# Quarter sums of the base weights made in the first phase and kept in DRAM; the second pair of token tiles takes seven products

## The chip, the cores and the metric

The kernel runs on one core of a Trainium2 chip, as one program. The metric is the device time in microseconds (us) of that core; lower is better. All data are fp32; matmul operands are split by hand into a high part (rounded to the type fp32r) and a low part (the rest), and a product is three fp32r matmuls: high by high, high by low, low by high.

## What is computed

A gated cross-attention block over `x` (4 batches of 512 tokens, width 1024), then a feed-forward part made of one base matrix and low-rank experts. The feed-forward part is what the change touches:

```python
x = x + tanh(g_xattn[0]) * xattn(layernorm(x), ctx, Wq, Wk, ...)      # first phase
x = x + tanh(g_ffn[0]) * ffn(layernorm(x), W_base, ...)               # last phase

def ffn(x, W_base, b_base, W_gate, W_thr, b_thr, A_w, B_w):
    base = einsum('bsd,od->bso', x, W_base) + b_base                  # 2048 x 1024 x 1024
    gate = softmax(xf @ W_gate.T)
    thr  = sigmoid(xf @ W_thr + b_thr[0]) * 0.125
    w    = relu(gate - thr), divided by its sum
    moe  = einsum('ner,ne,eor->no', xf @ A_w, w, B_w) * 2             # 8 experts, rank 16
    return base + moe
```

## The kernel before

**Stages.** One list of stages, `stages = first + last` (L334 to L440), is written out by hand. Every engine (TensorE, ScalarE, VectorE, GpSimd) and the DMA queue of SyncE walks the same list and does its own part of each stage, in that order; semaphores join them. So the place of a stage in the list fixes what is queued behind what on every engine.

**First phase (`first`).** In order: keys from the context (stages `k`, `k_out`, `k_low`, with the weights `wkf`, whose eight regions `r_wk` lie behind the context `ct`, L122); the products of the query weights with themselves (`g`, two sweeps of eight steps, brought out of PSUM by `g_out` into `gram`: ScalarE writes the high part, VectorE the low part); keys times query weights (`m`, eight rows, brought out by `m_out`); then for each of the four batches the row products `y` (eight per batch), scores, softmax and `attend`. Beside them run `x_stat` (statistics of the 16 token tiles of `x`, each loaded by SyncE two `x_stat` stages ahead, L788), and for batch `b` the chain `load_xt` (2 MB of transposed `x` in four quarters), `z` (VectorE scales a quarter, L1166), `zh` (ScalarE rounds it), `zl` (VectorE takes the rest, L1172). For batch 0 this chain stands inside the second `g` sweep; `load_xt` 0 waits until all key products are done (`p_k`, L797), because `x` transposed lies where `ct` and `wkf` lay. Row `m` r waits for `m_out` r-3 (L620), since three PSUM banks turn; `mr` 1, behind the first `y`, waits for the fourth `z` (L521).

**Last phase (`last`, L386 on).** The 2048 tokens are eight pairs of 128-token tiles. A pair p starts with `hd` (expert and gate logits, L701), takes its products with the base matrix, adds the expert part (`fin`), and is stored. The matrix is cut into quarters B11, B12, B21, B22 (1 MB each). A plain pair takes eight products (`PLAIN_PRODUCTS`), each of 12 matmuls of 128x512. Any other pair takes seven (`PRODUCTS`), with four sums of token quarters (s1 to s4) and four sums of weight quarters: T1 = B12 - B11, T2 = B22 - T1, T3 = B22 - B12, T4 = B21 - T2. `PLAIN = 2`: pairs 0 and 1 are plain, pairs 2 to 7 take seven. The token sums for the next pair are made by ScalarE and VectorE during the pair before (`zt`, `sum_high`, `sum_low`).

**Where the T's came from.** At the end of the first phase and in pairs 0 and 1 SyncE loads the raw quarters into the slots of the T's and a second copy beside them (`w_load`, L826). VectorE (T1, T2; L1326) and GpSimd (T4, T3; L1493) subtract half by half, ScalarE rounds the high half (`split`, L1053), VectorE takes the low (L1334). All this stands between the products of pairs 0, 1 and 2:

```python
PRODUCTS = [("P1", "a11", "B11", "A", True), ("P2", "a12", "B21", "B", True), ("P6", "s2", "T2", "A", False),
            ("P5", "s1", "T1", "C", True), ("P7", "s3", "T3", "A", False), ("P3", "s4", "B22", "C", False),
            ("P4", "a22", "T4", "D", True)]
```

Of the kernel before, what the change touches and what calls it, by code (L numbers as in the profile page):

```python
# [43 lines left out]
def build(nc, x, xt, ctx, ctxt, wq, wk, wb, hd, bt, vec, fn_w, b_base, scal, out):  # L44
# [9 lines left out]
    B = 4  # L54
# [10 lines left out]
    PLAIN = 2  # L65
# [3 lines left out]
    with ExitStack() as stack:  # L69
# [15 lines left out]
        def own(name, shape, dt=F32):  # L85
            n = WORD
            for s in shape[1:]:
# [33 lines left out]
                    for h, n in enumerate(("xth", "xtl")))  # L121
# [11 lines left out]
        EARLY, LATE = 2 * TPB, 3 * TPB  # L133
# [14 lines left out]
        xs = [at(f"xs{i}", [P, D], F32, o) for i, o in enumerate((r_kt + 2 * ROW, r_kt + 3 * ROW, r_xa, r_xa + ROW))]  # L148
# [7 lines left out]
        wh, wl, w_raw, w_tmp = ({op: at(f"{n}_{op}", [P, KH, HALF], dt, o + h * SLOT // 2) for op, o in w_at.items()}  # L156
                                for n, dt, h in (("wh", F32R, 0), ("wl", F32R, 1), ("wr", F32, 1), ("wx", F32, 0)))
# [162 lines left out]
        for p in range(NP):  # L320
# [8 lines left out]
            for i, (n, z, *_) in enumerate(products(p)):  # L329
                if all(z != z_ for _, z_, *_ in products(p)[i + 1:]):  # L330
# [14 lines left out]
        for r in range(KB):  # L345
            first += [("m", r), ("m_out", r)] + [("x_stat", EARLY + r - 2)] * (1 < r < 6)
        first += [("load_xt", 1), ("load_fn", 0), ("load_xa", 0), ("load_xa", 1), ("load_bb",)]
        for b in range(B):
            for j in range(FB):
# [10 lines left out]
                if b == 0 and j > 3:  # L360
                    first.append(("x_stat", LATE + j - 4))
# [20 lines left out]
        first += [("zt", 0, "a22"), ("load_xs", 1, 0), ("load_xs", 1, 1),  # L382
# [4 lines left out]
        for p in range(NP):  # L387
# [3 lines left out]
            if p + 1 < NP:  # L391
                q = p + 1
                if p == 0:
                    ahead = {0: [("xn", t0)], 1: [("stat", t1), ("bias", t0)], 3: [("zt", 1, "a11")],
                             4: [("zt", 1, "a12"), ("xn", t1)], 6: [("zt", 1, "a21"), ("bias", t1)], 7: [("zt", 1, "a22")]}
                elif plain(p):
                    ahead = {0: [("stat", t0), ("xn", t0)], 1: [("stat", t1)],
                             3: [("zt", q, "a21"), ("zt", q, "a22"), ("xn", t1), ("sum_high", q, "s1"), ("bias", t0)],
                             6: [("zt", q, "a11"), ("sum_high", q, "s3"), ("sum_high", q, "s2"), ("sum_low", q, "s1"),
                                 ("sum_low", q, "s3")],  # L400
                             7: [("zt", q, "a12"), ("sum_low", q, "s2"), ("sum_high", q, "s4"), ("bias", t1)]}
                else:
                    ahead = {0: [("attend", t0)] * attends + [("stat", t0)],
                             1: [("attend", t1)] * attends + [("xn", t0), ("stat", t1)],
                             3: [("zt", q, "a21"), ("zt", q, "a22"), ("xn", t1), ("sum_high", q, "s1"), ("bias", t0)],
                             4: [("zt", q, "a11"), ("sum_high", q, "s3"), ("sum_high", q, "s2"), ("sum_low", q, "s1"),
                                 ("sum_low", q, "s3")],
                             5: [("zt", q, "a12"), ("sum_low", q, "s2"), ("sum_high", q, "s4"), ("bias", t1)],
                             6: [("sum_low", q, "s4")]}
            t = 2 * p  # L410
            if p == 0:
                last += [("hd", 0, 0), ("w_load", "T4"), ("tops", B - 1), ("norms", B - 1),
                         ("gates", 0), ("stat", 2)]
                extra = {0: [("weights", 3), ("chosen", 0), ("hd", 0, 1), ("gates", 1), ("shares", 3), ("split", "B22", 0), ("fn_norm", 3),
                             ("chosen", 1)],
                         1: [("split", "B22", 1), ("mt", 0)],
                         2: [("pt", 3), ("load_bt",), ("fn_split", 3)], 3: [], 4: [("sum", "T1", 0)],
                         5: [("mt", 1), ("fn_low", 3), ("sum", "T1", 1)], 6: [("bt",), ("sum", "T2", 0)], 7: [("sum", "T2", 1)]}
            else:
                last += [("hd", p, 0), ("gates", t), ("hd", p, 1), ("gates", t + 1), ("chosen", t), ("chosen", t + 1)]  # L420
                extra = {2: [("mt", t), ("mt", t + 1)]} if attends else {1: [("mt", t)], 2: [("mt", t + 1)]}
                if plain(p):
                    extra = {0: [("split", "T1", 0), ("split", "T1", 1), ("sum", "T4", 0), ("sum", "T4", 1)],
                             1: [("mt", t), ("mt", t + 1)], 2: [("split", "T2", 0)], 3: [("w_load", "T3")],
                             4: [("split", "T2", 1)], 5: [("split", "T4", 0)], 6: [],
                             7: [("sum", "T3", 0), ("sum", "T3", 1)]}
                elif p == PLAIN:
                    extra = {0: [("sum_low", p, "s4")], 1: [("mt", t), ("mt", t + 1), ("split", "T3", 0)], 2: [("split", "T3", 1)], 4: [("split", "T4", 1)]}
# [52 lines left out]
        def tensor(pe):  # L481
# [27 lines left out]
            for stage, *i in stages:  # L509
# [234 lines left out]
        def sync(sp):  # L744
# [42 lines left out]
            for stage, *i in stages:  # L787
# [6 lines left out]
                elif stage == "load_xt":  # L794
                    b, = i
                    if b == 0:
                        sp.wait_ge(p_k, FB)  # L797
                    elif b == 1:
                        sp.wait_ge(p_m, KB)
                    else:  # L800
# [81 lines left out]
        def scalar(act):  # L882
# [195 lines left out]
        def vector(dve):  # L1078
# [20 lines left out]
            for stage, *i in stages:  # L1099
# [217 lines left out]
                elif stage == "sum" and i[0] not in POOL_SUMS:  # L1317
                    op, part = i
                    ks = slice(2 * part, 2 * part + 2)
                    dve.wait_ge(ld_w[op], 32 if op in ("T2", "T3") else 16)  # L1320
                    if op == "T1":
                        dve.wait_ge(ld_w["T2"], 32)
                    elif op != "T3":
                        dve.wait_ge(v_wt, W_SUMS[{"T2": "T1", "T4": "T2"}[op], part])
                    less = {"T1": w_tmp["T2"], "T2": w_raw["T1"], "T3": w_tmp["T3"], "T4": w_raw["T2"]}[op]
                    dve.tensor_tensor(w_raw[op][:, ks, :], w_raw[op][:, ks, :], less[:, ks, :],  # L1326
                                      ALU.subtract).then_inc(v_wt, 1)
                elif stage == "split":
# [3 lines left out]
                    if op == "T2":  # L1332
                        dve.wait_ge(g_wt, W_SUMS["T4", part])
                    dve.tensor_tensor(wl[op][:, ks, :], w_raw[op][:, ks, :], wh[op][:, ks, :].bitcast(F32),  # L1334
                                      ALU.subtract).then_inc(v_wl, 1)
# [96 lines left out]
        def gpsimd(pool):  # L1432
# [17 lines left out]
            for stage, *i in stages:  # L1450
# [35 lines left out]
                elif stage == "sum" and i[0] in POOL_SUMS:  # L1486
                    op, part = i
                    ks = slice(2 * part, 2 * part + 2)
                    pool.wait_ge(ld_w[op], 32 if op == "T3" else 16)
                    if op == "T4":  # L1490
                        pool.wait_ge(v_wt, W_SUMS["T2", part])
                    less = {"T3": w_tmp["T3"], "T4": w_raw["T2"]}[op]
                    pool.tensor_tensor(w_raw[op][:, ks, :], w_raw[op][:, ks, :], less[:, ks, :],  # L1493
# [73 lines left out]
```

## Time and profile before

| what | value |
|---|---|
| time, median of 3 runs | 486.79 us (485.83 to 488.88) |
| the profiled execution | 486.12 us |
| its span, first to last instruction | 484.2 us |
| TensorE matmul busy | 476.3 us, 98% of the span |
| VectorE busy | 343.5 us, 71% |
| ScalarE, GpSimd busy | 165.0 us, 126.2 us |
| TensorE clock granted | 1.000 on average |
| moved by DMA | 71.80 MB, 56.69 read from and 14.68 written to DRAM |

In the profile PE is TensorE's matmuls, DVE is VectorE, ACT is ScalarE, POOL is GpSimd, SPq is the DMA queue of SyncE. A time line gives the start of an instruction or of a run of equal ones, then the time it took. Matmuls overlap each other, so what a matmul costs is read from the distance between starts and not from its own duration.

### The profile page before, as it was taken

How to read it: one execution, taken by the hardware profiler on the slowest of the kernel's cores; microseconds unless marked ns; L12 is line 12 of the kernel's file. 1: busy time of each engine (PE TensorE's matmuls, PEld its weight loads, DVE VectorE, ACT ScalarE, POOL GpSimd, SP SyncE). 2: the span in 40 equal slices, each digit the busy share in tenths (PEclk: the TensorE clock that was granted, in tenths of full speed). 3: DMA queues.
4: the chain of work that ended last, by engine and by line, in shares of the span. 5: the costliest groups of instructions: out<-in, count | busy, mean ns of one | idle time of the engine just before them, and what ended most of it. 6: DMA issues, size and time to landing. Idle time of an engine off the chain costs nothing.

```text
span 484.2 us, 6865 instructions
## 1 busy us (share of the span) xinstructions
PE 476.3 (98%) x2470; PEld 404.2 (83%) x2470; DVE 343.5 (71%) x721; ACT 165.0 (34%) x339; POOL 126.2 (26%) x113
## 2 busy tenths in 40 slices
PE   8999999999999999999999999989999999999997
PEld 7888899998888888888788888868888888888885
DVE  1359669555777758679977985988677678777742
ACT  3757213311314213126326236244241421414300
POOL 1012020003263342345153425424040401305000
PEclk9999999999999999999999999999999999999999
DMA  8962272029742566556678054140503122050202
GB/s 273 409 275 89 87 261 87 1 88 318 246 154 64 202 212 238 217 213 226 219 279 372 2 173 175 43 130 2 174 1 131 44 71 104 1 173 2 87 1 87
DMA packets 20816, 71.80 MB, mean 148 GB/s; under 512 B 2480, under 2 KB 4528, under 8 KB 19504
## 3 DMA queue, kind: packets, MB, share of 16 engines
q1 hardware_dynamic: 20640, 71.35, 41.0%
q8 instruction: 20, 0.33, 0.3%
q14 instruction: 12, 0.10, 0.1%
q10 hardware_dynamic: 144, 0.02, 0.0%
HBM read 56.69 MB, written 14.68 MB: 147 GB/s over the span
## 4 chain that ended last, share of the span: by engine, by line
PE 89%; DVE 6%; DMA 2%; issue 2%; ACT 0%; SPq 0%; DVEq 0%; ACTq 0%
PE bank L602 10%; PE bank L721 10%; PE bank L725 10%; PE bank L723 10%; PE bank L638 6%; PE bank L640 6%; PE bank L639 6%; PE bank L573 4%; PE bank L701 4%; PE bank L492 3%; DVE wl_B L1334 2%; DMA out_dram<-xs 2%; PE bank L624 2%; PE bank L623 2%; PE bank L625 2%
## 5 line engine op out<-in xcount | busy, mean ns | idle before, releaser
L1448 POOL TENSOR_TENSOR small<-small,tiny 128x1 f32<-128x1 f32 (+2 forms) x25 | 23.7, 947 | 149.0 <-DVE small L1095 125.3
L638 PE MATMUL bank<-xth,gram 128*128 128x512 f32 x144 | 57.4, 398 | 0.0
L640 PE MATMUL bank<-xtl,gram 128*128 128x512 f32 x144 | 56.3, 391 | 0.0
L639 PE MATMUL bank<-xth,gram 128*128 128x512 f32 x144 | 56.1, 390 | 0.0
L721 PE MATMUL bank<-wh_B,zh 128*128 128x512 f32 x136 | 55.1, 405 | 0.0
L1422 DVE SCALAR_TENSOR_TENSOR xs<-bank,tiny,xs 128x512 f32<-128x512 f32 x56 | 40.1, 746 | 20.7 <-PE bank L725 14.7
L725 PE MATMUL bank<-wh_B,zl 128*128 128x512 f32 x136 | 53.5, 393 | 0.0
L723 PE MATMUL bank<-wl_B,zh 128*128 128x512 f32 x136 | 53.3, 392 | 0.0
L1476 POOL TENSOR_TENSOR sq_sum<-sq_sum,sq 128x512 f32<-128x512 f32 x24 | 32.0, 1332 | 62.6 <-DVE sq L1270 62.6
L1512 POOL TENSOR_TENSOR xs<-xs,bb 128x1024 f32<-128x1024 f32 x16 | 38.8, 2428 | 10.0 <-ACT zn L962 7.4
L721 PE MATMUL bank<-wh_T,zh 128*128 128x512 f32 x96 | 39.3, 410 | 2.0 <-DVE wl_T L1334 1.7
L1270 DVE SCALAR_TENSOR_TENSOR sq<-bank,gsm,xz 128x512 f32<-128x512 f32 x32 | 23.9, 747 | 22.2 <-PE bank L640 20.6
L725 PE MATMUL bank<-wh_T,zl 128*128 128x512 f32 x96 | 37.7, 393 | 0.0
L723 PE MATMUL bank<-wl_T,zh 128*128 128x512 f32 x96 | 37.7, 392 | 0.0
L919 ACT ACTIVATE xth<-xz 128x1024 fp32r<-128x1024 f32 x16 | 17.0, 1061 | 49.1 <-DVE xz L1166 49.1
L640 PEld LDWEIGHTS bank<-xtl,gram 128*128 128x128 f32 x144 | 27.0, 188 | 5.8
L701 PE MATMUL bank<-hw,zh 128*128 128x276 f32 x128 | 31.2, 335 | 0.6 <-DVE zl L1198 0.6
L639 PEld LDWEIGHTS bank<-xth,gram 128*128 128x128 f32 x144 | 27.1, 188 | 5.3
L638 PEld LDWEIGHTS bank<-xth,gram 128*128 128x128 f32 x144 | 27.1, 188 | 5.2
L962 ACT ACTIVATE zn<-xs,small 128x1024 f32<-128x1024 f32 x16 | 19.9, 1242 | 32.3 <-POOL small L1504 32.3
L725 PEld LDWEIGHTS bank<-wh_B,zl 128*128 128x128 f32 x136 | 25.5, 188 | 5.9
L723 PEld LDWEIGHTS bank<-wl_B,zh 128*128 128x128 f32 x136 | 25.7, 189 | 4.9
(191 smaller groups left out, 1089.8 us busy)
## 6 DMA issues: line engine op xcount, KB each, us to landing
xst<-x_dram SPq DMA_DIRECT2D x16, 512.0 KB, 3.7
xz<-xt_dram SPq DMA_DIRECT2D x16, 512.0 KB, 6.4
out_dram<-xs SPq DMA_DIRECT2D x14, 512.0 KB, 2.6
xa<-x_dram SPq DMA_DIRECT2D x12, 512.0 KB, 3.2
x<-xa SPq DMA_DIRECT2D x12, 512.0 KB, 2.6
xs<-x SPq DMA_DIRECT2D x12, 512.0 KB, 3.9
wq_raw<-wq_dram SPq DMA_DIRECT2D x8, 512.0 KB, 14.5
wr_B<-wb_dram SPq DMA_DIRECT2D x4, 1024.0 KB, 6.8
```

The lines of the kernel that those rows point to most:

```text
L602: done = pe.matmul(dst, blocks[left][:, row, :], blocks[right][:, cols.start:cols.stop:cols.step, :], start=n == f == left == right == 0, ...
L638: pe.matmul(acc[:, :], gram[:, g, 0, :], xth[b % 2][:, r, :], start=r == ROWS[j][0], stop=False)
L639: pe.matmul(acc[:, :], gram[:, g, 1, :], xth[b % 2][:, r, :], start=False, stop=False)
L640: done = pe.matmul(acc[:, :], gram[:, g, 0, :], xtl[b % 2][:, r, :], start=False, stop=r == ROWS[j][-1])
L701: pe.matmul(acc[:, 0:2 * HEAD], zh[z][:, k, :], hw[w][:, k, :], start=n == k == 0, stop=False, skip_group_check=True)
L721: pe.matmul(acc[:, :], zh[z][:, k, :], wh[op][:, k, :], start=opens and k == 0, stop=False, skip_group_check=True)
L723: pe.matmul(acc[:, :], zh[z][:, k, :], wl[op][:, k, :], start=False, stop=False, skip_group_check=True)
L725: done = pe.matmul(acc[:, :], zl[z][:, k, :], wh[op][:, k, :], start=False, stop=k == KH - 1, skip_group_check=True)
L1270: dve.scalar_tensor_tensor(out=sq[n % 2][:, :], in0=bank[Y_BANKS[n % 3]][:, :], scalar=wb2[:, j:j + 1], in1=xz[b % 2][:, j, :], op0=ALU.ad ...
L1422: dve.scalar_tensor_tensor(out=xs[slot][:, half(h)], in0=bank[C_BANK[n_bank]][:, :], scalar=tg[:, 1:2], in1=xs[slot][:, half(h)], op0=ALU. ...
L1476: pool.tensor_tensor(sq_sum[:, :], addend[:, :], sq[j % 2][:, :], ALU.add).then_inc(g_qsum, 1)
L1512: pool.tensor_tensor(xs[slot][:, :], xs[slot][:, :], bb[:, :], ALU.add).then_inc(g_x1, 1)
```

## The change

The first phase now makes the T's. The stages `t_load` (a raw quarter into the regions of the key weights as they come free), `t_sum` (one subtraction of 128x2048; T1, T2, T4 on VectorE, T3 on GpSimd), `split` (T1, T3, T2 into high and low, two halves each on ScalarE and VectorE) and `t_keep` (store to DRAM: high and low of T1, T3, T2, the sum alone of T4) are spread over both `g` sweeps. `w_load` fetches the parts back in the last phase (T1, T2, T3 as two ready parts of 1 MB, T4 as one, split as before). `PLAIN` is 1: pair 1 takes seven products. `load_xt` 0 now waits until all seven stores have landed, and the `z`, `zh`, `zl` of batch 0 move from the second `g` sweep between the rows of `m`. `x_stat` 8 and 9 stay beside `m`; 10 and 11 move beside the `y` of batch 0, where six of them now stand. The two tiles of pair 1 change their order and slots.

```diff
-    PLAIN = 2
+    PLAIN = 1
-        EARLY, LATE = 2 * TPB, 3 * TPB
+        EARLY, LATE = 2 * TPB, 2 * TPB + NXA
+        T_FROM = {"T1": "B11", "T3": "B12", "T2": "B22", "T4": "B21"}
+        t_at = {"T1": r_wk[0], "T3": r_wk[FB - 1] + ROW, "T2": r_wk[2], "T4": r_wk[4]}
+        t_raw, t_low = ({op: at(f"{n}_{op}", [P, KH, HALF], dt, o) for op, o in t_at.items()}
+                        for n, dt in (("t_raw", F32), ("t_low", F32R)))
+        t_high = {op: at(f"t_high_{op}", [P, KH, HALF], F32R, o) for op, o in (("T1", r_wk[6]), ("T3", r_x0), ("T2", r_wk[6]))}
+        t_dram = {op: [nc.dram_tensor(f"{op}_{part}", [P, KH, HALF], F32) for part in ("high", "low")[:1 + (op != "T4")]]
+                  for op in T_FROM}
...
-                 ("k_low", 2), ("k_low", 3), ("g", 0, 3), ("x_stat", 0), ("wq", 5), ("k", 5), ("x_stat", 1), ("g", 0, 4),
-                 ("wq", 6), ("k_out", 4), ("k_out", 5), ("k_low", 4), ("k_low", 5), ("wq", 7), ("g", 0, 5), ("x_stat", 2),
-                 ("g", 0, 6), ("x_stat", 3), ("g", 0, 7), ("k", 6), ("k", 7), ("g_out", 0), ("load_xt", 0),
-                 ("k_out", 6), ("k_out", 7), ("k_low", 6), ("k_low", 7), ("g", 1, 0), ("x_stat", 4), ("g", 1, 1),
-                 ("x_stat", 5), ("tanh",), ("g", 1, 2), ("k_norm",), ("x_stat", 6), ("mr", 0), ("g", 1, 3),
-                 ("x_stat", 7), ("z", 0, 0), ("zh", 0, 0), ("g", 1, 4), ("z", 0, 1), ("zh", 0, 1), ("zl", 0, 0),
-                 ("g", 1, 5), ("z", 0, 2), ("zh", 0, 2), ("zl", 0, 1), ("g", 1, 6), 
-                 ("z", 0, 3), ("zh", 0, 3), ("zl", 0, 2), ("g", 1, 7), ("zl", 0, 3), ("g_out", 1)]
+                 ("k_low", 2), ("k_low", 3), ("g", 0, 3), ("t_load", "T1"), ("t_load", "T3"), ("t_load", "T2"), ("x_stat", 0),
+                 ("wq", 5), ("k", 5), ("x_stat", 1), ("g", 0, 4), ("t_load", "T4"), ("wq", 6), ("k_out", 4), ("k_out", 5),
+                 ("k_low", 4), ("k_low", 5), ("wq", 7), ("g", 0, 5), ("x_stat", 2), ("g", 0, 6), ("x_stat", 3), ("t_sum", "T1"),
+                 ("g", 0, 7), ("t_sum", "T3"), ("k", 6), ("k", 7), ("g_out", 0),
+                 ("k_out", 6), ("k_out", 7), ("k_low", 6), ("k_low", 7), ("t_sum", "T2"), ("x_stat", 4), ("split", "T1", 0),
+                 ("split", "T1", 1), ("x_stat", 5), ("t_keep", "T1"), ("t_sum", "T4"), ("g", 1, 0), ("split", "T3", 0),
+                 ("split", "T3", 1), ("t_keep", "T4"), ("t_keep", "T3"), ("g", 1, 1), ("tanh",),
+                 ("g", 1, 2), ("k_norm",), ("x_stat", 6), ("mr", 0), ("g", 1, 3), ("split", "T2", 0), ("split", "T2", 1),
+                 ("t_keep", "T2"), ("g", 1, 4), ("x_stat", 7), ("g", 1, 5), ("load_xt", 0), ("g", 1, 6), ("g", 1, 7), ("g_out", 1)]
         for r in range(KB):
-            first += [("m", r), ("m_out", r)] + [("x_stat", EARLY + r - 2)] * (1 < r < 6)
+            first += [("m", r), ("m_out", r)]
+            first += [("zh", 0, r - 3)] * (3 <= r < 7)
+            first += {0: [("x_stat", EARLY)], 1: [("x_stat", EARLY + 1)], 2: [("z", 0, 0)],
+                      3: [("z", 0, 1)], 4: [("z", 0, 2), ("zl", 0, 0)], 5: [("z", 0, 3), ("zl", 0, 1)],
+                      6: [("zl", 0, 2)], 7: [("zl", 0, 3)]}[r]
...
-                if b == 0 and j > 3:
-                    first.append(("x_stat", LATE + j - 4))
+                if b == 0 and j > 2:
+                    first += [("x_stat", LATE + j - 3)] + [("x_stat", NT - 1)] * (j == FB - 1)
...
-                         1: [("split", "B22", 1), ("mt", 0)],
-                         2: [("pt", 3), ("load_bt",), ("fn_split", 3)], 3: [], 4: [("sum", "T1", 0)],
-                         5: [("mt", 1), ("fn_low", 3), ("sum", "T1", 1)], 6: [("bt",), ("sum", "T2", 0)], 7: [("sum", "T2", 1)]}
+                         1: [("mt", 0), ("split", "B22", 1)],
+                         2: [("pt", 3), ("load_bt",), ("fn_split", 3)], 3: [("w_load", "T3")], 4: [("fn_low", 3)],
+                         5: [("mt", 1), ("bt",)]}
...
-                if plain(p):
-                    extra = {0: [("split", "T1", 0), ("split", "T1", 1), ("sum", "T4", 0), ("sum", "T4", 1)],
-                             1: [("mt", t), ("mt", t + 1)], 2: [("split", "T2", 0)], 3: [("w_load", "T3")],
-                             4: [("split", "T2", 1)], 5: [("split", "T4", 0)], 6: [],
-                             7: [("sum", "T3", 0), ("sum", "T3", 1)]}
-                elif p == PLAIN:
-                    extra = {0: [("sum_low", p, "s4")], 1: [("mt", t), ("mt", t + 1), ("split", "T3", 0)], 2: [("split", "T3", 1)], 4: [("split", "T4", 1)]}
+                if p == PLAIN:
+                    extra = {0: [("sum_low", p, "s4")], 1: [("mt", t), ("mt", t + 1)], 2: [("split", "T4", 0)], 3: [("split", "T4", 1)]}
...
                 elif stage == "load_xt":
                     b, = i
                     if b == 0:
-                        sp.wait_ge(p_k, FB)
+                        for op in T_FROM:
+                            sp.wait_ge(ld_w[op], T_KEPT[op])
...
+                elif stage == "t_keep":
+                    op, = i
+                    if op == "T4":
+                        sp.wait_ge(v_wt, T_SUMS[op])
+                        sp.dma_start(t_dram[op][0].ap(), t_raw[op][:, :, :]).then_inc(ld_w[op], 16)
+                        continue
+                    sp.wait_ge(a_wh, SPLITS[op, 1])
+                    sp.dma_start(t_dram[op][0].ap(), t_high[op][:, :, :].bitcast(F32)).then_inc(ld_w[op], 16)
+                    sp.wait_ge(v_wl, SPLITS[op, 1])
+                    sp.dma_start(t_dram[op][1].ap(), t_low[op][:, :, :].bitcast(F32)).then_inc(ld_w[op], 16)
...
+                        if op == "T2":
+                            act.wait_ge(ld_w["T1"], T_KEPT["T1"])
+                        else:
+                            act.wait_ge(p_k, FB)
+                        act.activation(t_high[op][:, ks, :], t_raw[op][:, ks, :], ACT.Copy).then_inc(a_wh, 1)
```

## Rows read from the trace of the kernel before

**Rows 1.** The page: the span, and the busy line of TensorE's matmuls
```profile
span 484.2 us, 6865 instructions
PE 476.3 (98%) x2470; PEld 404.2 (83%) x2470; DVE 343.5 (71%) x721; ACT 165.0 (34%) x339; POOL 126.2 (26%) x113
```
**Rows 2.** Who TensorE waited for: us in total, times, longest
```profile
PE bank L721 <- DVE wl_T L1334: 1.7, 1, 1.7
...
PE bank L701 <- DVE zl L1198: 0.6, 1, 0.6
...
PE bank L721 <- DVE xs L1422: 0.3, 1, 0.3
```
**Rows 3.** Time line of TensorE: first matmul of pairs 1, 2, 3, 4
```profile
277.03 0.29 PE L701 MATMUL bank<-hw,zh 128*128 128x276 f32 x1
...
307.78 0.29 PE L701 MATMUL bank<-hw,zh 128*128 128x276 f32 x1
...
339.11 0.29 PE L701 MATMUL bank<-hw,zh 128*128 128x276 f32 x1
...
367.06 0.29 PE L701 MATMUL bank<-hw,zh 128*128 128x276 f32 x1
```
**Rows 4.** The page's groups of instructions: product matmuls (busy, mean ns)
```profile
L721 PE MATMUL bank<-wh_B,zh 128*128 128x512 f32 x136 | 55.1, 405 | 0.0
```
**Rows 5.** Time line of TensorE: `k` 6 and 7, `g` sweep 2, `m` 0, 2, 6, `y`
```profile
53.09 7.07 PE L573 MATMUL bank<-ct,wkf 128*128 128x256 f32 x32
59.81 1.35 PE L602 MATMUL bank<-wqh 128*128 128x512 f32 x6
...
85.82 0.28 PE L623 MATMUL bank<-kth,wqh 128*128 128x258 f32 x1
...
91.60 0.28 PE L623 MATMUL bank<-kth,wqh 128*128 128x258 f32 x1
...
103.11 0.28 PE L623 MATMUL bank<-kth,wqh 128*128 128x258 f32 x1
...
108.89 0.39 PE L638 MATMUL bank<-xth,gram 128*128 128x512 f32 x1
```
**Rows 6.** Time line of VectorE: `g_out` 0, `x_stat` 4, `g_out` 1
```profile
53.30 3.85 DVE L1126 SCALAR_TENSOR_TENSOR gram<-bank,gram 128x128 fp32r<-128x128 f32 x19 [0.94 <-ACT gram L938]
...
64.01 1.27 DVE L1151 BATCH_NORM_STATS2 small<-xst 128x6 f32<-128x512 f32 x2
...
86.06 3.45 DVE L1126 SCALAR_TENSOR_TENSOR gram<-bank,gram 128x128 fp32r<-128x128 f32 x17 [1.81 <-ACT gram L938]
```
**Rows 7.** Time lines of VectorE (three rows), then of GpSimd (two rows)
```profile
285.40 2.35 DVE L1334 TENSOR_TENSOR wl_T<-wr_T,wh_T 128x1024 fp32r<-128x1024 f32 x2
...
304.49 4.35 DVE L1218 TENSOR_TENSOR zl<-zr,zh 128x512 fp32r<-128x512 f32 x2
...
326.87 0.75 DVE L1422 SCALAR_TENSOR_TENSOR xs<-bank,tiny,xs 128x512 f32<-128x512 f32 x1
...
299.67 5.82 POOL L1493 TENSOR_TENSOR wr_T<-wr_T,wx_T 128x1024 f32<-128x1024 f32 x2 [1.58 <-DMA wx_T<-wb_dram]
...
326.96 4.76 POOL L1512 TENSOR_TENSOR xs<-xs,bb 128x1024 f32<-128x1024 f32 x2
```
**Rows 8.** Two stretches with all engines, DMA share, GB/s; landings of L825, L764
```profile
60.00:69.00 9.00, 9.00 (x55) 8.08 (x53) 6.60 (x15) 1.80 (x5) 1.68 (x2) 1.00 0.83 289
249.00:263.00 14.00, 14.00 (x75) 11.83 (x74) 11.50 (x40) 7.23 (x19) 2.71 (x5) 1.00 1.00 406
...
DMA to landing us min/median/max: 2.6/2.6/4.6
...
DMA to landing us min/median/max: 4.3/6.4/9.5
```
**Rows 9.** Time lines of ScalarE (`bt` in pair 0) and TensorE (its `fin`)
```profile
268.31 1.05 ACT L1064 ACTIVATE bth<-bt_raw 128x1024 fp32r<-128x1024 f32 x1
...
274.18 0.48 PE L739 MATMUL bank<-bth,mth 128*128 128x512 f32 x1
```

More of the change, by code:

```diff
@@ L147, in build @@
         xa = [at(f"xa{i}", [P, D], F32, r_xa + i * ROW) for i in range(NXA)]
-        xs = [at(f"xs{i}", [P, D], F32, o) for i, o in enumerate((r_kt + 2 * ROW, r_kt + 3 * ROW, r_xa, r_xa + ROW))]
+        xs = [at(f"xs{i}", [P, D], F32, o) for i, o in enumerate((r_kt + 2 * ROW, r_kt + 3 * ROW, r_xa + ROW, r_xa))]
         zn = at("zn", [P, D], F32, r_kx)
@@ L268, in build @@
             sem(f"g_{n}") for n in ("const", "ctx", "rs", "ksum", "krs", "mr", "qsum", "rq", "fnrs", "wt", "off", "x1"))
+        T_RAW, T_KEPT, T_BACK = 16, {op: 32 + 16 * (op != "T4") for op in T_FROM}, {op: 48 + 32 * (op != "T4") for op in T_FROM}
         CONSTS = 8
@@ L381, in build @@
                 first.append(("load_xt", b + 2))
-        first += [("zt", 0, "a22"), ("load_xs", 1, 0), ("load_xs", 1, 1),
+        first += [("zt", 0, "a22"), ("load_xs", 1, 1), ("load_xs", 1, 0),
                   ]
@@ L393, in build @@
                 if p == 0:
[L394 to L398, printed above, removed]
+                    ahead = {0: [("xn", t0)], 1: [("stat", t1), ("bias", t0)],
+                             3: [("zt", q, "a21"), ("zt", q, "a22"), ("xn", t1), ("sum_high", q, "s1")],
                              6: [("zt", q, "a11"), ("sum_high", q, "s3"), ("sum_high", q, "s2"), ("sum_low", q, "s1"),
-                                 ("sum_low", q, "s3")],
-                             7: [("zt", q, "a12"), ("sum_low", q, "s2"), ("sum_high", q, "s4"), ("bias", t1)]}
+                                 ("sum_low", q, "s3"), ("bias", t1)],
+                             7: [("zt", q, "a12"), ("sum_low", q, "s2"), ("sum_high", q, "s4")]}
                 else:
@@ L445, in build @@
         SPLITS = {key: n + 1 for n, key in enumerate((s[1], s[2]) for s in stages if s[0] == "split")}
-        POOL_SUMS = ("T4", "T3")
-        W_SUMS = {key: n + 1 for n, key in enumerate((s[1], s[2]) for s in stages if s[0] == "sum" and s[1] not in POOL_SUMS)}
-        W_SUMS.update({key: n + 1 for n, key in enumerate((s[1], s[2]) for s in stages if s[0] == "sum" and s[1] in POOL_SUMS)})
+        WHOLE_KEPT = ("B11", "B21", "B12", "B22", "T4")
+        T_SUMS = {key: n + 1 for n, key in enumerate(s[1] for s in stages if s[0] == "t_sum" and s[1] != "T3")}
         def nq(b, f):
@@ L1316, in vector @@
                                       ALU.subtract).then_inc(v_fn, 1)
[L1317 to L1320, printed above, removed]
+                elif stage == "t_sum" and i[0] != "T3":
+                    op, = i
+                    left, right = {"T1": ("T3", "T1"), "T2": ("T2", "T1"), "T4": ("T4", "T2")}[op]
                     if op == "T1":
[L1322 to L1326, printed above, removed]
+                        dve.wait_ge(ld_w["T1"], T_RAW)
+                        dve.wait_ge(ld_w["T3"], T_RAW)
+                    elif op == "T2":
+                        dve.wait_ge(g_wt, 1)
+                        dve.wait_ge(v_wt, T_SUMS["T1"])
+                    else:
+                        dve.wait_ge(ld_w["T4"], T_RAW)
+                        dve.wait_ge(v_wt, T_SUMS["T2"])
+                    dve.tensor_tensor(t_raw[op][:, :, :], t_raw[left][:, :, :], t_raw[right][:, :, :],
                                       ALU.subtract).then_inc(v_wt, 1)
@@ L1331, in vector @@
                     dve.wait_ge(a_wh, SPLITS[op, part])
[L1332 to L1335, printed above, removed]
+                    if op in WHOLE_KEPT:
+                        dve.tensor_tensor(wl[op][:, ks, :], w_raw[op][:, ks, :], wh[op][:, ks, :].bitcast(F32),
+                                          ALU.subtract).then_inc(v_wl, 1)
+                    else:
+                        if op in ("T1", "T2"):
+                            dve.wait_ge(v_wt, T_SUMS[{"T1": "T2", "T2": "T4"}[op]])
+                        dve.tensor_tensor(t_low[op][:, ks, :], t_raw[op][:, ks, :], t_high[op][:, ks, :].bitcast(F32),
+                                          ALU.subtract).then_inc(v_wl, 1)
                 elif stage == "head_w":
@@ L1485, in gpsimd @@
                     root(fn_rs(b), fn_tmp(b)).then_inc(g_fnrs, 1)
[L1486 to L1493, printed above, removed]
+                elif stage == "t_sum" and i[0] == "T3":
+                    pool.wait_ge(ld_w["T2"], T_RAW)
+                    pool.wait_ge(v_wt, T_SUMS["T1"])
+                    pool.tensor_tensor(t_raw["T3"][:, :, :], t_raw["T2"][:, :, :], t_raw["T3"][:, :, :],
                                        ALU.subtract).then_inc(g_wt, 1)
```

42 lines of the change are left out of this document (25 added, 17 removed).

## The prediction

> **What bounds the kernel now.** I read the page first: matmuls are busy for 476.3 of 484.2 us [rows 1]. TensorE is the bound nearly everywhere, so only two things can make the kernel faster: fewer matmuls, or fewer of the few gaps. The list of waits names the gaps: five in all, three of them in the last phase, 1.7 us for the low part of a T, 0.6 us for a low token part, 0.3 us for an eviction [rows 2]. The time line of TensorE gives the price of a pair as the distance between first matmuls of `hd` [rows 3]: pair 1 (plain) 307.78 - 277.03 = 30.75; pair 2 (the first with seven products) 339.11 - 307.78 = 31.33; pair 3, 367.06 - 339.11 = 27.95. Pair 2 should cost what pair 3 costs; it costs 3.38 more, since all three gaps lie in it (2.6 us, and some 0.8 for getting going again behind them).
>
> **What is taken away.** Pair 1 becomes a pair of seven products: 30.75 to 27.95, a gain of 2.80 us. That is one product of 12 matmuls, 0.233 us each. The mean duration of such a matmul, 0.405 us [rows 4], would promise 4.9 us; it is wrong to multiply it, because consecutive matmuls overlap, and I take the distance.
>
> The Trainium skill (TensorE: Matmul & The Clock Gate, Back-to-back issue gap) gives about 131 ns for each matmul of 512 columns in a stream with weight loads. By that figure a product would be 1.6 us and the sum below 1.2 us less gain. The trace does not agree (233 ns between starts), and the measurement decides.
>
> Pair 2 loses its 3.38 if none of its three gaps returns. The 1.7 was a late half of a T, made by ScalarE and VectorE between products; T1, T2 and T3 now come ready from DRAM. The 0.6 came from VectorE held up: two `sum_low` of it took 4.35 us in pair 1, while GpSimd ran its T3 sums (5.82 us) and a bias [rows 7]. The sums are gone from there. The 0.3 followed from the 0.6. So the last phase gains 2.80 + 3.38 = 6.18 us, call it 6.2. Its lower bound is the product alone, 2.8.
>
> **What is added to the last phase.** Pair 0 now makes the token sums of pair 1. VectorE loses four half T sums of 128x1024 and one low of 128x512, and gains seven token sums and lows of 128x512, half the size: no more work than before. The transition 2 to 3, with nearly the same list, shows no gap [rows 2, 3]. Loads in the queue before `bt`: B22 1, T1 2, T2 2, T4 1 = 6 MB where there were 5. One more is 1.05/0.406 = 2.6 us at the full rate [rows 8]. `bt` had landed when ScalarE began on it at 268.31; late by 2.6 it is there by 270.9, its two steps of 1.1 and 1.2 us end at 273.2, `fin` wants them at 274.18 [rows 9]. Hidden, by 1.0 us at the least. In pair 1 the two halves of T4 cost VectorE 2 x 1.2 us [rows 7], before P4, the last product; GpSimd's bias steps (two in 4.76 us, [rows 7]) may hold each up by up to 2.4 us. What waits behind them is the low part and s1 of the token tiles; TensorE wants that bank only two transposes later, one product and more away. I take 0 and keep 2.4 for the range.
>
> **What is added to the first phase.** On VectorE: three sums of 128x2048 and six lows of 128x1024. A pair of lows takes 2.35 us [rows 7]; a sum of 2048 is the same size, so 3 x 2.35 + 3 x 2.35 = 14.1 us. Away from the `g` sweeps go `z` and `zl` of batch 0, eight steps of 128x1024, 9.4 by the same row. All of it lies beside matmuls, if two dates hold.
>
> First date: sweep 2 begins at 59.81 and its fourth piece needs the last bank of `g_out` 0. `g_out` 0 on VectorE ran 53.30 to 57.1 [rows 5, 6]. The T1 sum goes ahead of it, 52.4 to 54.7, so `g_out` 0 ends at 58.5: slack 1.3 us even to the first piece. GpSimd makes T3 then (two halves of 2.4, so 4.8 us). Would it hold `g_out` up? An eviction of the same kind (one input in PSUM, one in SBUF) took its normal 0.75 us at 326.87 right beside GpSimd's bias [rows 7], while two-SBUF-input steps suffered. `g_out` is of the first sort: 0.
>
> Second date: from 64.01 VectorE does T2 sum 2.35, `x_stat` 4 1.4 (estimate from its 1.27 row), T1 lows 2.35 (70.1), `x_stat` 5 (71.5), T4 sum (73.9), T3 lows (76.2), the key norm (77.7), `x_stat` 6 (79.1). SyncE stores T1 only behind `x_stat` 5, at 71.7, behind one 0.52 MB load. 2.6 MB at 406 GB/s are 6.5 us, and a store of 0.52 MB lands in 2.6 us of which 1.3 is transfer, so 1.3 on top: T1 kept at 79.5. Only then may ScalarE round T2, whose high part takes T1's place; VectorE follows to 83.1, `x_stat` 7 ends at 84.5. `g_out` 1 began at 86.06 and ended at 89.5; `m` 2 needs it at 91.60 [rows 5, 6]. Slack 1.5 + 2.1 = 3.6 us.
>
> **The long chain.** Seven stores of 1.05 MB and the loads of two `x` tiles (8.39 MB) follow each other without a pause from about 72: 20.7 us at 406 GB/s, plus 1.3: all kept at 94.0. Then `load_xt` 0. Its first quarter lands 4.3 to 6.4 us after [rows 8]; one `x` load still stands in front. I take 4.9: 98.9. Batch 0's first `z` follows (1.2), then `m_out` 3 (0.5): 100.6. `m` 6 waits for that at 103.11 [rows 5], so the quarter may land as late as 101.3. Slack 2.4 us. Behind it `z`, `zl`, `m_out` alternate and end with the last `z` at 106.4 (`mr` 1 wants it at about 109.6), and the first `zl` at 104.7 (`y` wants it at 108.89 [rows 5]). The price is 0, the slack thin; from 101.3 on, each us of lateness is paid in full.
>
> The Trainium skill (HBM Reference, Specifications) gives an effective 358 GB/s per core of DRAM bandwidth, and says that a core alone measures above it. The trace agrees with the second half (406 GB/s over 14 us, loads). By 358 the quarter would land at 101.6 and the stall be 0.3 us.
>
> `x_stat` 10 and 15 add 2.9 us to VectorE within batch 0's `y` steps, which need it one bank in three; hidden.
>
> **Sum.** Span 484.2 - 6.2 + 0 = 478.0 us. The profiled execution took 486.12 with span 484.2, 1.9 more; the median of the runs is 486.79, 0.7 above that execution. Against the median: 486.8 - 6.2 = **480.6 us**, 1.3% less.
>
> **The rivals.**
> R1, the chain is somewhat late. Bound by the stretch 60 to 69: 289 GB/s at a share of 0.83, so 348 at full share [rows 8]. 8.39 MB are then 24.1 us, and with a landing of 6.4 the quarter comes at 72 + 24.1 + 1.3 + 6.4 = 103.8: stall 2.5, time 483.1. At 289 itself, 108.7, stall 7.4, time 488.0. For it: no row shows 7 MB of stores in a row. Against it: the 406 of the loads.
> R2, the other side: the return through DRAM is the new bound, slower than before. If stores pay their 2.6 us per 0.52 MB one after another with no overlap [rows 8], seven take 36.4 and two loads 5.2, the quarter lands at 72 + 41.6 + 4.9 = 118.5, `m` 6 waits 17.2, time 480.6 + 17.2 = 497.8. It decides from a landing of 107.5 on (101.3 + 6.2), and is over 1% slower from 112.4. Against it: loads and stores are spread over the same 16 engines, and loads do overlap.
> R3, the gaps of pair 2 stay or move into pair 1 (T4 against the bias, evictions late behind the statistics): only the product is gained, 2.8, up to 0.6 of it lost again: 484.0 to 484.6.
>
> **How the numbers follow.** Forecast (479.6 to 481.9) 0.51; R1 0.27, most of it between 482 and 486; R2 0.07; R3 0.12; still faster, because the first phase or the `y` steps lose small gaps too, 0.03. 1% of 486.8 is 4.9 us (about what a measurement of this kernel can tell from no change), so under 481.9 is faster, over 491.7 slower. Faster: 0.51 + 0.03 and 0.01 of R1's mild end = 0.55. Slower: R2 0.07 and 0.01 of R1. Same: 0.37. The range 479.6 to 486.8 leaves out the 0.03 below, R2, and 0.04 of R1: 0.14.
>
> **What would show it.** TensorE: pairs 1 and 2 both 27.9 long, and no wait in them; no wait in sweep 2; `m` 6 without a gap. DMA: a block of stores from 72 to 94 at some 400 GB/s, T1 kept at 79 to 80. VectorE: first `z` at about 99. Wrong if a wait for `z`, `mk` or a key part stands before `m` 6 (R1, R2: its length is the stall), if `g_out` 1 starts after 88.2, or if pair 1 or 2 is over 28.5 (R3).

## The result, and the profile after

| kernel | median, range, runs | ratio to before, 95% interval |
|---|---|---|
| before, beside it | 486.5 us (485.83 to 488.88, 4) | 1 |
| after | 480.81 us (480.54 to 481.96, 4) | 0.9879 (0.9841 to 0.9917) |
| after, measured again with the experiments | 480.11 us (479.99 to 480.21) | 0.9865 (0.9848 to 0.9882), before 486.43 |

The change makes the kernel 1.2 to 1.4% faster, some 5.7 to 6.3 us; the median forecast was 480.6 us. The profile shown below is of the slowest of the first four runs, 481.96 us with a span of 480.0; the spans of the other three were 478.5 to 479.0, and that of the second measurement's profiled run, called "after, second trace" here, is 478.2 (forecast: 478.0). Where the 1.8 us between the two traces come from is told below.

The page of after: the span, the busy line, and what the DMA moved.

```profile
span 480.0 us, 6880 instructions
...
PE 473.2 (99%) x2458; PEld 402.1 (84%) x2458; DVE 347.2 (72%) x731; ACT 167.7 (35%) x343; POOL 121.0 (25%) x110
...
DMA packets 22545, 84.39 MB, mean 176 GB/s; under 512 B 2672, under 2 KB 4720, under 8 KB 19696
...
HBM read 61.93 MB, written 22.02 MB: 175 GB/s over the span
```

Against [rows 1]: 12 matmuls fewer, the one product of pair 1, and 3.1 us less of busy TensorE. VectorE has 3.7 us more, GpSimd 5.2 less. DMA moves 12.6 MB more, and none of TensorE's waits below is put down to one of the added transfers.

Waits of TensorE, after (us in total, times, longest), then the same view of the second trace:

```profile
PE bank L666 <- POOL sq_sum L1514: 1.7, 1, 1.7
PE bank L514 <- DVE idle L1128: 1.2, 1, 1.2
PE bank L687 <- DVE xa L1394: 0.3, 1, 0.3
PE bank L570 <- DMA wk<-wk_dram: 0.2, 1, 0.2
```

```profile
PE bank L514 <- DVE idle L1128: 1.2, 1, 1.2
PE bank L687 <- DVE xa L1394: 0.2, 1, 0.2
PE bank L570 <- ACT ct L931: 0.2, 1, 0.2
PE bank L570 <- DMA wk<-wk_dram: 0.2, 1, 0.2
```

The three waits of [rows 2] are gone in both. There is a new one of 1.7 us in one of them, in the first phase, before the norms of batch 0.

Time line of TensorE in the second trace: the first matmul of pairs 1, 2, 3 and 4, which answers [rows 3].

```profile
277.23 0.29 PE L708 MATMUL bank<-hw,zh 128*128 128x276 f32 x1
...
305.16 0.29 PE L708 MATMUL bank<-hw,zh 128*128 128x276 f32 x1
...
333.11 0.29 PE L708 MATMUL bank<-hw,zh 128*128 128x276 f32 x1
...
361.06 0.29 PE L708 MATMUL bank<-hw,zh 128*128 128x276 f32 x1
```

Pairs 1 and 2 are now 27.93 and 27.95 us long, where they were 30.75 and 31.33: 6.20 us less, in both traces of after. Pair 1 begins at 277.23, 0.20 later than before: without the wait of 1.7 us the first phase pays almost nothing for making the T's.

The first phase on VectorE in after: sum of T1, `g_out` 0, sum of T2, lows of T1, lows of T2, `g_out` 1, `x_stat` 9, the first `z`.

```profile
52.70 2.29 DVE L1360 TENSOR_TENSOR t_raw_T<-t_raw_T,t_raw_T 128x2048 f32<-128x2048 f32 x1
54.91 3.84 DVE L1157 SCALAR_TENSOR_TENSOR gram<-bank,gram 128x128 fp32r<-128x128 f32 x19
...
64.42 2.28 DVE L1360 TENSOR_TENSOR t_raw_T<-t_raw_T,t_raw_T 128x2048 f32<-128x2048 f32 x1
...
68.05 2.31 DVE L1372 TENSOR_TENSOR t_low_T<-t_raw_T,t_high_T 128x1024 fp32r<-128x1024 f32 x2
...
81.72 2.36 DVE L1372 TENSOR_TENSOR t_low_T<-t_raw_T,t_high_T 128x1024 fp32r<-128x1024 f32 x2 [2.61 <-ACT t_high_T L1084]
...
86.48 3.45 DVE L1157 SCALAR_TENSOR_TENSOR gram<-bank,gram 128x128 fp32r<-128x128 f32 x17 [0.76 <-ACT gram L966]
...
96.52 1.29 DVE L1182 BATCH_NORM_STATS2 small<-xst 128x6 f32<-128x512 f32 x2 [3.40 <-DMA xst<-x_dram]
...
99.83 1.22 DVE L1197 TENSOR_TENSOR xz<-xz,bank 128x1024 f32<-128x1024 f32 x1 [1.43 <-DMA xz<-xt_dram]
```

The queue of SyncE in after: the stores of T1 and of T2, then the load of the first transposed `x`, which waits until all stores have landed. And two stretches with all engines (last three columns: TensorE clock, DMA share, GB/s).

```profile
71.96 0.43 SPq L867 DMA_DIRECT2D T_high<-t_high_T  x1
...
84.11 0.32 SPq L869 DMA_DIRECT2D T_low<-t_low_T  x1
...
95.42 1.76 SPq L773 DMA_DIRECT2D xz<-xt_dram  x4
```

```profile
71.90:94.00 22.10, 22.10 (x152) 20.79 (x152) 15.78 (x40) 5.78 (x21) 2.04 (x2) 1.00 0.98 389
82.00:94.00 12.00, 12.00 (x92) 11.64 (x91) 9.40 (x30) 4.40 (x20) 1.01 (x1) 1.00 1.01 413
```

The long chain is there and keeps its dates: `g_out` 0 ends at 58.75 (forecast 58.5), the first store is issued at 71.96 (72), all parts are kept at 95.4 (94.0), the first `z` starts at 99.83 (98.9), and TensorE does not notice.

### The profile page after: what moved, and what is told of

It is laid out like the page before. It is cut to its first block, busy times and chain, and to the rows that moved or that the text cites. A ratio compares the mean times of both kernels' runs of the same rounds, so it can differ in the third digit from the quotient of the medians.

```text
span 480.0 us, 6880 instructions
## 1 busy us (share of the span) xinstructions
PE 473.2 (99%) x2458; PEld 402.1 (84%) x2458; DVE 347.2 (72%) x731; ACT 167.7 (35%) x343; POOL 121.0 (25%) x110
## 4 chain that ended last, share of the span: by engine, by line
PE 86%; DMA 6%; DVE 6%; issue 1%; SPq 1%; POOL 1%; ACT 0%; DVEq 0%
PE bank L730 11%; PE bank L734 11%; PE bank L732 11%; PE bank L609 10%; PE bank L708 5%; PE bank L580 4%; PE bank L645 4%; PE bank L647 4%; PE bank L646 4%; PE bank L499 3%; DMA xst<-x_dram 3%; PE bank L710 2%; DVE wl_B L1367 2%; PE bank L631 2%; PE bank L630 2%; PE bank L632 2%
## 5 line engine op out<-in xcount | busy, mean ns | idle before, releaser
L1486 POOL TENSOR_TENSOR small<-small,tiny 128x1 f32<-128x1 f32 (+2 forms) x25 | 21.7, 869 | 161.7 <-DVE small L1126 137.3
L1460 DVE SCALAR_TENSOR_TENSOR xs<-bank,tiny,xs 128x512 f32<-128x512 f32 x60 | 43.2, 747 | 21.5 <-PE bank L734 15.3
L730 PE MATMUL bank<-wh_B,zh 128*128 128x512 f32 x116 | 47.0, 405 | 0.0
L730 PE MATMUL bank<-wh_T,zh 128*128 128x512 f32 x112 | 45.9, 410 | 0.0
L734 PE MATMUL bank<-wh_B,zl 128*128 128x512 f32 x116 | 45.6, 393 | 0.0
L732 PE MATMUL bank<-wl_B,zh 128*128 128x512 f32 x116 | 45.4, 391 | 0.0
L734 PE MATMUL bank<-wh_T,zl 128*128 128x512 f32 x112 | 44.1, 393 | 0.0
L732 PE MATMUL bank<-wl_T,zh 128*128 128x512 f32 x112 | 44.0, 393 | 0.0
L710 PE MATMUL bank<-hw,zl 128*128 128x138 f32 x128 | 29.0, 226 | 0.0
L734 PEld LDWEIGHTS bank<-wh_B,zl 128*128 128x128 f32 x116 | 21.8, 188 | 5.0
```

The costliest lines, as they stand in the source:

```text
L710: done = pe.matmul(acc[:, 0:HEAD], zl[z][:, k, :], hw[w][:, k, 0:HEAD], start=False, stop=n == 1 and k == KH - 1, skip_group_check=True)
L730: pe.matmul(acc[:, :], zh[z][:, k, :], wh[op][:, k, :], start=opens and k == 0, stop=False, skip_group_check=True)
L732: pe.matmul(acc[:, :], zh[z][:, k, :], wl[op][:, k, :], start=False, stop=False, skip_group_check=True)
L734: done = pe.matmul(acc[:, :], zl[z][:, k, :], wh[op][:, k, :], start=False, stop=k == KH - 1, skip_group_check=True)
L1460: dve.scalar_tensor_tensor(out=xs[slot][:, half(h)], in0=bank[C_BANK[n_bank]][:, :], scalar=tg[:, 1:2], in1=xs[slot][:, half(h)], op0=ALU. ...
```

## The experiments

The second run of after (the control below), the later loads, the plain pair 1 and the two stores stand against 486.43 us, the cut T3 sums and the four stores against 486.74.

**After, once more.** No edit.

> The changed kernel again, as the mate of the other runs of this call. Theory: 5.5 to 6 us less than before; the wait of TensorE for sq_sum at the norms of batch 0 (1.7 us in the profile after) is there again, because the load of x tile 12, issued at 121, lands 13 us later. Rival: the wait was chance of one execution, and is gone here.

Measured: 480.11 us, the waits and pair starts shown above. The wait for the norms did not come back, so it is not a fixed part of the price. What brings it about is there in both executions, though. First after, then the second trace: VectorE's time line at `x_stat` 12.

```profile
133.98 1.29 DVE L1182 BATCH_NORM_STATS2 small<-xst 128x6 f32<-128x512 f32 x2 [4.14 <-DMA xst<-x_dram]
```

```profile
132.22 1.29 DVE L1182 BATCH_NORM_STATS2 small<-xst 128x6 f32<-128x512 f32 x2 [2.35 <-DMA xst<-x_dram]
```

The `x` tile of `x_stat` 12 was issued at 120.94 and 120.49, behind the transposed `x` of batch 1, `fn_raw`, `xa` and `bb`, which are issued from 110 to 116. It landed 13.0 us later in one execution and 11.7 in the other. VectorE waits for it in both, with its steps on the results of batch 0's `y` queued behind. In the later case `x_stat` 12 starts 1.76 us later, GpSimd's last sum of those results ends 1.73 later (142.97 against 141.24), and TensorE waits 1.70 us:

```profile
143.12 1.02 PE L666 MATMUL bank<-tiny,sq_sum 128*128 128x2 f32 x8 [1.70 <-POOL sq_sum L1514]
```

**The block of loads behind the `y` of batch 0.**

```diff
-        first += [("load_xt", 1), ("load_fn", 0), ("load_xa", 0), ("load_xa", 1), ("load_bb",)]
+        first += [("load_xt", 1), ("load_fn", 0)]
...
+                if b == 0 and j == 6:
+                    first += [("load_xa", 0), ("load_xa", 1), ("load_bb",)]
```

> The changed kernel with one edit: the loads of the two xa tiles and of the bias row (1.5 MB) are issued behind the seventh y step of batch 0 and not ahead of the first. Theory A (the load of x tile 12 queues behind them, x_stat 12 waits 4.1 us for it, and the sq and sq_sum behind it come late to the norms): tile 12 lands about 4 us earlier, the wait of x_stat 12 falls under 1 us, TensorE's wait at the norms (1.7 us) goes, 1.7 to 2.2 us less than the changed kernel. Rival B (VectorE has two more x_stat, 2.9 us, before the last y step of batch 0, whenever they come): a wait of 1 us or more stays at the norms, gain under 0.7 us.

Measured: 479.91 us (479.84 to 479.99), ratio 0.9862 (0.9847 to 0.9877). `x_stat` 12 waits for nothing now:

```profile
129.64 1.27 DVE L1184 BATCH_NORM_STATS2 small<-xst 128x6 f32<-128x512 f32 x2
```

That the block in front made the tile late is shown. Against the control it is worth only 0.2 us, and neither forecast came true as it stands, since the control had no wait at the norms either. What it gives is room: GpSimd's last sum ends at 140.11, 1.0 us before TensorE's matmul of the norms (141.15), where the control had 0.15. It is the fastest version that was run, by little.

**Pair 1 plain again, the T's still from DRAM.** The core of the edit; the token stages and slots of pair 1 go back to those of before.

```diff
-    PLAIN = 1
+    PLAIN = 2
...
-                         2: [("pt", 3), ("load_bt",), ("fn_split", 3)], 3: [("w_load", "T3")], 4: [("fn_low", 3)],
+                         2: [("pt", 3), ("load_bt",), ("fn_split", 3)], 3: [], 4: [("fn_low", 3)],
...
+                if plain(p):
+                    extra = {1: [("mt", t), ("mt", t + 1)], 3: [("w_load", "T3")]}
```

> The changed kernel with pair 1 plain again (eight products), so only the making and keeping of the weight sums in the first phase is left of the change. Theory: pair 1 is 30.75 long, pair 2 27.95 without its three gaps; 2.8 us more than the changed kernel, 2.5 to 3.2 less than before. Rival: the gaps of pair 2 do not come from weight sums made between the products, but from the step from a plain pair to one of seven; then pair 2 stays at 30 to 31.3 and the kernel is within 1 us of before.

Measured: 483.11 us (482.57 to 483.9), ratio 0.9927 (0.9914 to 0.9941). Pairs 1, 2 and 3 begin at:

```profile
276.77 0.29 PE L713 MATMUL bank<-hw,zh 128*128 128x276 f32 x1
...
307.50 0.29 PE L713 MATMUL bank<-hw,zh 128*128 128x276 f32 x1
...
335.47 0.29 PE L713 MATMUL bank<-hw,zh 128*128 128x276 f32 x1
```

Pair 1 is 30.73 us long, pair 2 27.97. This splits the gain: 486.43 - 483.11 = 3.3 us for the gaps of pair 2, 483.11 - 480.11 = 3.0 us for the product; together 6.3, the whole of it. The forecast had 3.38 and 2.80; the measured parts are each uncertain by some 0.7 us, so they agree with it but do not tell which part is the larger.

**Before, without GpSimd's T3 sums.** The edit in the `sum` stage of GpSimd:

```diff
-                    pool.tensor_tensor(w_raw[op][:, ks, :], w_raw[op][:, ks, :], less[:, ks, :],
+                    n = 4 if op == "T3" else HALF
+                    pool.tensor_tensor(w_raw[op][:, ks, 0:n], w_raw[op][:, ks, 0:n], less[:, ks, 0:n],
```

> The kernel before, with GpSimd's two T3 sums cut from 1024 columns (two of 512 in each row block) to 4 in each: it leaves out nearly the whole sum B22 - B12, so the products with T3 are not the reference's. Theory (GpSimd's T3 sums of 5.8 us stretch VectorE's low steps in pair 1, and the 0.6 us wait for a low token part and the 0.3 us wait for an eviction follow from that): the two low steps that took 4.35 us take about 2.4, the waits of 0.6 and 0.3 are gone, the wait of 1.7 us for the low part of a T stays, pair 2 is 30.0 to 30.5 us long where it was 31.33, and the time is 1.0 to 1.3 us under the kernel before (485.1 to 485.5). Rival (the lateness comes from VectorE's own list, GpSimd only runs beside it): the waits of 0.6 and 0.3 stay, pair 2 keeps 31.3, the time is that of before, 486.4.

Measured: 483.51 us (483.27 to 483.6), ratio 0.9933 (0.9917 to 0.995): 3.2 us less, near the whole 3.38 and not the 1.0 to 1.3 that I expected. My theory was right that VectorE is stretched by GpSimd's work and wrong on how much hangs on it. Time line of VectorE, at the place of [rows 7]; then two of TensorE's waits, the first of which lies ahead of pair 0 (at 242, in before too) and the second in pair 2.

```profile
304.79 1.29 DVE L1218 TENSOR_TENSOR zl<-zr,zh 128x512 fp32r<-128x512 f32 x2
...
325.02 0.69 DVE L1198 TENSOR_TENSOR zl<-bank,zh 128x512 fp32r<-128x512 f32 x1
```

```profile
PE bank L680 <- DVE xa L1356: 0.6, 1, 0.6
PE bank L721 <- DVE wl_T L1334: 0.2, 1, 0.2
```

Two low steps take 1.29 us where they took 4.35 [rows 7]. GpSimd's time line says beside what: in before (first row) and here (the other two).

```profile
305.45 2.85 POOL L1512 TENSOR_TENSOR xs<-xs,bb 128x1024 f32<-128x1024 f32 x1
```

```profile
299.91 1.35 POOL L1494 TENSOR_TENSOR wr_T<-wr_T,wx_T 128x8 f32<-128x8 f32 x2 [1.49 <-DMA wx_T<-wb_dram]
301.22 2.39 POOL L1513 TENSOR_TENSOR xs<-xs,bb 128x1024 f32<-128x1024 f32 x1
```

In before the low steps (304.49 to 308.84) have only the last 1.0 us of the T3 sums beside them (which end at 305.49) and then the whole bias step, which had stood behind the sums; here the bias is done at 303.61, before they begin. So the cut took both neighbours away, and how much of the stretch each of them makes is not shown. The lateness of 2 to 3 us then ran down VectorE's list: in before the statistics of the next tile stood at 319.13, 11.35 us into pair 2, and here at 317.20, 9.11 us into it. The statistics go through GpSimd to ScalarE, whose `xn` stands ahead of the rounding of the last half of T3, so the low part of that half was late too: 1.7 us before, 0.2 here. The sum of T3 was not itself the late part: it was there at 305.49, and ScalarE rounded its last half at 323.66. Pair 2 is 28.41 us long (308.09 to 336.50), 2.9 less than before and 0.5 more than pair 3. One cause, three waits.

**Two more stores in the chain, then four.** Copies of T2's low part, 1.05 MB each, to DRAM regions that nobody reads; the load of the first transposed `x` waits for them too. The core of the edit:

```diff
+                    for more in t_more if op == "T2" else ():
+                        sp.dma_start(more.ap(), t_low[op][:, :, :].bitcast(F32)).then_inc(ld_more, 16)
```

> The changed kernel with two more stores of 1 MB behind those of T2, which the load of batch 0 waits for too: 2.1 MB, 5.2 us at 406 GB/s. Theory (in the profile after the first z starts at 99.8; m 6 can take it until about 101.7): first z at about 105, TensorE waits 3 to 3.5 us in the m rows in all, 3 to 3.5 us more than the changed kernel. Rival (the chain has more slack than that, or VectorE and the banks catch up): under 1 us more. Second rival (stores queue worse than loads): over 5 us more.

Measured, two stores: 482.94 us (482.37 to 484.83, three runs), ratio 0.9934 (0.9911 to 0.9956), 2.8 us over the control, a little under what was expected.

> After, with four more stores of 1.05 MB behind the last one of T2, for which the load of the first transposed x waits too. Two such stores made the tile of x_stat 9 land 5.0 us later and cost 2.7 us. Theory (a chain with some 2.4 us of slack, and beyond it each us of lateness is paid in full): 4.2 MB are 10.4 us more, so the wait before m 5 or m 6 is 7.5 to 8.5 us and the time 487.9 to 489, slower than before. Rival (part of the lateness is made good behind the wait, or the stores overlap better when more stand in the queue): the wait is 5 to 6 us and the time 485 to 486.5. Either way it shows where the return through DRAM would have turned the gain into nothing.

Measured, four stores: 489.75 us (489.27 to 490.24, two runs), ratio 1.0063 (1.0042 to 1.0083), slower than before. In each trace the tile of `x_stat` 9 (VectorE) and the wait of TensorE; two stores, then four:

```profile
101.49 1.28 DVE L1187 BATCH_NORM_STATS2 small<-xst 128x6 f32<-128x512 f32 x2 [8.21 <-DMA xst<-x_dram]
...
103.42 0.39 PE L632 MATMUL bank<-kth,wqh 128*128 128x258 f32 x1 [2.45 <-DVE gsm L1173]
```

```profile
106.61 1.29 DVE L1187 BATCH_NORM_STATS2 small<-xst 128x6 f32<-128x512 f32 x2 [13.92 <-DMA xst<-x_dram]
...
108.55 0.58 PE L632 MATMUL bank<-kth,wqh 128*128 128x258 f32 x1 [8.16 <-DVE gsm L1173]
```

Each 2.1 MB make the tile 5.0 to 5.1 us later (96.50, 101.49, 106.61), that is 410 to 420 GB/s. TensorE waits 2.45 and 8.16 us, so the slack was 2.5 and 2.0. In the trace with four stores `m` 0 began at 85.80, 0.4 before that of after (86.23), which is nearly the difference. Between two and four stores the lateness rose by 5.1 and the wait by 5.7: paid in full, as forecast.

The time rose by more than the wait, though: pair 1 begins at 286.29, 9.06 after the control's 277.23, with 8.16 waited and a start 0.4 earlier, so 1.3 are something else. The stretches of the four-store kernel (TensorE busy first, granted clock third from the end) show it:

```profile
104.00:108.00 4.00, 0.00 (x0) 0.00 (x0) 1.35 (x3) 0.00 (x0) 0.00 (x0) 0.58 0.48 148
108.00:112.00 4.00, 3.45 (x18) 3.45 (x19) 2.66 (x7) 0.91 (x1) 0.00 (x0) 0.57 1.01 363
112.00:116.00 4.00, 4.00 (x36) 4.00 (x35) 4.00 (x8) 2.89 (x6) 0.00 (x0) 1.00 0.23 91
```

The 0.58 and 0.57 are means of stretches in which the clock changes. Taken more finely, it is 1.00 from 100.40 to 104.50, 0.50 from 105.00 to 108.50, both with TensorE idle, still 0.50 from 108.55 to 111.00, its lower level (1.2 of 2.4 GHz), with TensorE at work again, and 1.00 from 112. So after 8 idle us TensorE does 18 matmuls in 3.45 us where 31 fit at the 9 per us of the next stretch: 13 / 9 = 1.4 us. In the kernel with two stores, idle for 2.45 us, the granted clock stayed 1.00.

## Why the prediction was right, point by point

**The sum.** 6.2 us were forecast; 6.3 were measured the second time and 5.7 the first, whose profiled execution has the wait of 1.7 us, which the forecast did not have. The two parts of the gain are right one by one: product 2.80 against 3.0 (pair 1: 2.82 shorter), gaps 3.38 against 3.3. The distance between pair starts was the right measure; the 405 ns of a matmul [rows 4] would have promised 4.9 for the product. The matmuls of a product stand 0.23 us apart in after too, not at the 131 ns of the Trainium skill (TensorE: Matmul & The Clock Gate, Back-to-back issue gap).

**The gaps of pair 2.** The step "The 1.7 was a late half of a T, made by ScalarE and VectorE between products" named the last link and missed the first. Cutting GpSimd's T3 sums took 1.5 of the 1.7 away. I had them as three waits with two causes; it was one, GpSimd's sums and bias beside VectorE's steps, to which the prediction put down the 0.6 and the 0.3 alone. It did not hurt the number, since the change takes the T sums out of the last phase altogether: that the reasons did not matter to the sum was luck.

**The added work in the last phase.** `bt` was forecast to be there by 270.9; in the first trace, where pair 1 begins 2.0 us later than before, ScalarE began on it at 271.37, after waiting 1.01 us for it, and `fin` came at 276.14: hidden. The T4 low halves in pair 1 took 1.22 and 2.91 us, the second held up by GpSimd's bias, 1.7 of the 2.4 allowed; TensorE had no wait there. R3 (gaps that stay or move) has nothing for it.

**First phase, first date.** `g_out` 0 took 3.84 us with GpSimd's T3 sum, 55.85 to 60.38, right beside it, as against 3.85 [rows 6]: the argument that an eviction with one input in PSUM does not suffer holds here. VectorE's own sum of T1 was not slowed either (2.29), but GpSimd's statistics step on 4 columns took 3.01 us beside it (1.02 at 127.00). GpSimd's time line:

```profile
52.87 3.01 POOL L1486 TENSOR_TENSOR ms<-small,tiny 128x4 f32<-128x4 f32 x1 [6.18 <-DVE small L1190]
55.85 4.53 POOL L1527 TENSOR_TENSOR t_raw_T<-t_raw_T,t_raw_T 128x2048 f32<-128x2048 f32 x1
```

**Second date.** T2's rounding began at 80.62 (forecast 79.5), its lows ended at 84.1, `g_out` 1 began at 86.48, 0.4 after [rows 6], like all of `m`, which began 0.4 later. No wait.

**The long chain.** All kept at 95.4, not 94.0. The rate of the stretch was 389 GB/s with 0.98 of the engines' time, against 406 [rows 8]: 8.39 MB in 21.6 us, 0.9 of the 1.4; the other 0.5 is not accounted for. The load of the first quarter then took 4.4 us, not 4.9. The slack was forecast as 2.4 (its own terms, 103.11 less 1.7, give 101.4 and so 2.5) and measured as 2.5. But it is not that of the first `z`: the link that broke was the tile of `x_stat` 9, behind the stores in the same queue, with `m_out` 2 behind it on VectorE and `m` 5 waiting for that. The number was near by some luck, as both loads are released by the same stores. R1 and R2 fall: seven stores overlap, and stores with loads move nearly as many bytes as loads alone. R2's turning point, a first quarter at 107.5, was placed well: between the kernels with two stores (first `z` at 104.69, 482.94 us) and with four (109.83, 489.75) a straight line, which is an estimate, gives 486.7 there, the time of before. By the Trainium skill's effective 358 GB/s per core (HBM Reference, Specifications) the chain would have been 1.9 us longer than at 389. The same section says that a core alone gets more, and there the trace agrees: 389 over 22 us and 413 over 12 us of stores and `x` loads.

**The step that failed.** The number came out right all the same. "`x_stat` 10 and 15 add 2.9 us to VectorE within batch 0's `y` steps, which need it one bank in three; hidden." I had counted the time of the instructions and not the arrival of what they read. `x_stat` 12 is now loaded behind the block described above and waits 2.4 to 4.1 us for its tile, which costs nothing in one execution and 1.7 us in another. It would have been found by following each moved stage's load through SyncE's queue.

What stays open: why the tile lands 1.3 us later in one execution than in the other. The DMA engines are busy in both (share 1.0) from 120 to 128, but move 253 and then 226 GB/s in the later case, 272 and then 352 in the other; what slows the same loads down is not shown. And whether this wait is behind the spread of after's times, 479.99 to 481.96, is only argued: two of its executions have a profile, the slowest with the wait and a faster one without.

## What to carry to other kernels

When several short waits stand in a row, look for the one late step at the head of the list that feeds them: here 5.8 us of sums on an engine that is 26% busy, and the step that they pushed back, cost 3.2 us on TensorE. Work on weights, which depends on no token, can be done where TensorE covers it and kept in DRAM, if the chain "store, landed, load, first use" is dated link by link, with each load that shares the queue; measure its slack by adding stores. Price a matmul by the distance between groups, and for a long wait look at the granted clock behind it: 8.2 us cost 1.4 more here, 2.45 us nothing.

## What the runs showed of the hardware that I had not expected

- Two VectorE steps of 128x512 with two SBUF inputs took 4.35 us beside GpSimd steps of the same sort and 1.29 us without. The two engines did not share evenly: a VectorE low of 128x1024 that began 0.57 us into GpSimd's bias took 2.91 us instead of 1.22, and GpSimd's step on 4 columns, begun 0.17 us into a VectorE sum, took 3.01 instead of 1.02, while that sum kept its 2.29. In both the step that began second paid more.
- Stores to DRAM and loads together ran at 389 GB/s over 22 us and 413 over 12 us of it on this one core, near the 406 of loads [rows 8].
- After 8.2 idle us TensorE restarted at 0.50 of its clock and lost some 1.4 us more; after 2.45 idle us it kept 1.00.
- A 0.52 MB load issued behind a block of loads landed 11.7 or 13.0 us after its issue, where the median of such a load in the kernel is 4.2 us.
